# The score fetch of a graph layer: one selection over two PSUM banks, TensorE filling four banks as two pairs

## The chip, the core and the metric

The kernel runs on one core of a Trainium2 chip. The metric is the device time of one execution in microseconds (us), so less is better. TensorE is the engine of the matrix products, VectorE (DVE) works element by element, ScalarE (ACT) computes functions and copies, GpSimd (POOL) here mostly gathers rows, and SyncE (SP) issues transfers. Each runs its own list of instructions in order and waits for the others on counting semaphores.

## The reference

The layer normalizes 3125 node rows of 256 numbers, adds to them a graph attention over 50,000 sorted edges and a second-order attention over all nodes, and ends in a mixture of eight experts of which each row uses two. The graph attention needs, for every edge, a score of its source node and of its destination node in each of four heads:

```python
h = (x @ W).reshape(N, HEADS, HEAD_DIM)
a_src = jnp.einsum('nhd,hd->nh', h, att_src)
a_dst = jnp.einsum('nhd,hd->nh', h, att_dst)
e = a_src[src] + a_dst[dst]
e = jax.nn.leaky_relu(e, NEG_SLOPE)
m = jax.ops.segment_max(e, dst, num_segments=N)
e = jnp.exp(e - m[dst])
```

The change lies in `a_src[src]`: the fetch of 4 source scores for each of 50,176 edges (padded), which the kernel does with matrix products and not with a gather.

## The kernel before

Node scores lie in `tsp`, split into three bf16 parts, with 25 tiles of nodes times 4 heads in the 100 columns. The edges are cut into 128 rows of `EP = 392`; `n` counts these rows. A source index is split into a low part (0 to 127) and a tile number. For a row `n` VectorE has made a one-hot of the low parts (`low_onehots(m)`, L1632, one operation for the 8 rows of group `m`). TensorE multiplies `tsp` by it, three products added up in one PSUM bank (L1180): 100 candidates for each edge, one for every tile and head. VectorE keeps the candidate whose tile is that of the edge and zeroes the others (L1741, the selection, written to one of 8 buffers `mskd`). TensorE then sums the 100 lines to 4 with `rsel` (L1189, `collect`), four rows at a time into quarters of a bank of its own.

TensorE works in 33 turns `i` of `JB = 4` rows: `candidates(i)` fills four banks, `collect(i - 1)` sums the four rows before, and after seven odd turns (`SIDE = (5, 9, 11, 13, 15, 17, 19)`) `side(k)` slips in a small product of another task through bank 5. Candidates rotate over banks 0 to 4: row `n` waits until row `n - 5` is selected (`s_fm`, one count for each selection). `s_fp` counts filled banks, `s_fq` collected turns.

VectorE runs over `n` in order. Ahead of the selections stand other jobs: the one-hot of the next group ahead of row 1 of every group of 8 (`n % FP == 1`), a chain of small operations on slot tables ahead of row 8 (`slot_tables`, L1654 to L1693), a conversion ahead of row 24 (`slot_locals`, L1697 to L1701), and the reading of side product `k` ahead of the row two behind the turn that follows it (`n % JB == 2`; L1706 for k=0, L1708, L1710, five operations L1714 to L1719 for k=3 and k=4, L1725 and L1726 for k=5 and k=6). All these rows `n` are of the form 8j + 2.

After each eight turns ScalarE copies the four sums of a quarter out of PSUM (L944) and SyncE stores them. After the last, SyncE loads all scores back by edge (L735). The scans for the maxima, the projections (L1256) and all that follows come behind the fetch on every engine.

Of the kernel before, what the change touches and what calls it, by code (L numbers as in the profile page):

```python
# [10 lines left out]
ALU = mybir.AluOpType  # L11
# [5 lines left out]
P = 128  # L17
# [3 lines left out]
GH, GD = 4, 64  # L21
MH, MD = 8, 32
NE, HID = 8, 1024
NT = -(-N // P)
# [13 lines left out]
EP = 392  # L38
# [17 lines left out]
JB = 4  # L56
# [67 lines left out]
def gps_layer(nc, x, src, dst, wcat, wgt, att_src, att_dst, gbias, bqkv, wpt, bproj, temp,  # L124
# [6 lines left out]
    def sem(name):  # L131
        return ctx.enter_context(nc.semaphore(name))
# [12 lines left out]
    with ctx:  # L145
# [35 lines left out]
        A = arena[:, :]  # L181
# [4 lines left out]
        def view(base, off, words, pat=None, **kw):  # L186
            v = base[:, off:off + words]
            return v.rearrange(pat, **kw) if pat else v
# [102 lines left out]
        FOFF = RG0  # L291
        FP = 2 * GH
        FM = 2 * JB
# [3 lines left out]
        LB = 4  # L297
        lob = [view(A, AP0 + u * NM // 2, NM // 2).bitcast(BF16) for u in range(LB)]
        hib = [view(A, AP0 + LB * NM // 2 + u * NM // 4, NM // 4).bitcast(U8) for u in range(LB)]
        mskd = [view(A, FOFF + u * EP, EP) for u in range(FM)]  # L300
# [3 lines left out]
        tsp = view(A, o, 3 * NT * GH // 2).bitcast(BF16).rearrange("p (s n) -> p s n", s=3)  # L304
        o += 150
        rsel = view(A, o, 60)
        hi_of = view(A, o + 60, 1)
# [55 lines left out]
        ps = ctx.enter_context(nc.psum_tensor("ps", [P, 8, 512], F32))  # L363
# [67 lines left out]
        s_fp = sem("candidate_scores")  # L431
        s_fm = sem("scores_selected")
# [685 lines left out]
        def _(pe):  # L1118
            MM, TR = nc.tensor.matmul, nc.tensor.transpose
# [7 lines left out]
            for k in range(KD):  # L1127
                for c in range(KD):
                    last = MM(ps[:, 7, k * AH:(k + 1) * AH], wgt_s[:, c, k * P:(k + 1) * P], att_s[:, c, :],
                              start=(c == 0), stop=(c == KD - 1))  # L1130
# [19 lines left out]
            for t in range(NT + 2):  # L1150
                if t < NT:
                    transpose_x(t)
                if t == 2:
                    pe.wait_ge(s_pairb, 1)
                    for c in range(NQC):
                        last = TR(ps[:, 6, c * MD:(c + 1) * MD], pairf[0:MD, c, :], identf[0:MD, 0:MD])
# [13 lines left out]
            def candidates(i):  # L1170

                if i % 2 == 0:
                    pe.wait_ge(s_ohl, i // 2 + 1)
                for c in range(JB):
                    n = i * JB + c
                    if n >= 5:
                        pe.wait_ge(s_fm, n - 4)
                    col = slice((n % FP) * EP, (n % FP + 1) * EP)
                    for s in range(3):
                        last = MM(ps[0:NT * GH, n % 5, 0:EP], tsp[:, s, :], lob[i // 2 % LB][:, col], start=(s == 0), stop=(s == 2))  # L1180
                    last.then_inc(s_fp, 1)

            def collect(i):
                q, k = i // FP, i % FP
                pe.wait_ge(s_fm, (i + 1) * JB)
                if k == 0 and q >= 2:
                    pe.wait_ge(s_fe, q - 1)
                for c in range(JB):
                    last = MM(ps[c * NQ:(c + 1) * NQ, 6 + q % 2, 0:EP], rsel[0:NT * GH, 28 - 4 * k:60 - 4 * k],  # L1189
                              mskd[(i * JB + c) % FM][0:NT * GH, :], start=(k == 0), stop=(k == FP - 1), skip_group_check=True)  # L1190
                last.then_inc(s_fq, 1)
# [26 lines left out]
            for i in range(NQ + 1):  # L1218
                if i < NQ:
                    candidates(i)  # L1220
                if i:
                    collect(i - 1)
                if i in SIDE:
                    side(SIDE.index(i))
            pe.wait_ge(s_w, 16 * 6)
            pe.wait_ge(s_fm, P)
            pe.wait_ge(s_sided, 7)


# [139 lines left out]
            for g in range(KD):  # L1369
                for c in range(NQC):  # L1370
                    last = TR(ps[:, 3 + g, c * P:(c + 1) * P], ftc[g][:, c * P:(c + 1) * P], identf[:, :])
            for c in range(2 * KD):
                last = TR(ps[:, 5, c * P:(c + 1) * P], lcb[:, c * P:(c + 1) * P], identf[:, :])
# [3 lines left out]
            for g in range(KD):  # L1377
                for c in range(NQC):
                    MM(ps[0:MD, 0, g * P:(g + 1) * P], pn[c][:, :], coef[g][:, c * P:(c + 1) * P], start=(c == 0), stop=False)
                last = MM(ps[0:MD, 0, g * P:(g + 1) * P], pn16[:, :], cf16[g], start=False, stop=True)  # L1380
# [75 lines left out]
            for n in range(ZR + 1):  # L1456
                r, c = n // NQC, n % NQC
# [44 lines left out]
            for k in range(TOPK):  # L1502
                pe.wait_ge(s_slots, k + 1)
                for t in range(NT):
                    n = P if t < NT - 1 else TAIL
                    last = MM(ps[:, 3, 0:2 * NJ], lo1[k][0:n, t, :], slotv[k][0:n, t, :, :].rearrange("p v j -> p (v j)"),
                              start=(k == 0 and t == 0), stop=(k == TOPK - 1 and t == NT - 1))
# [40 lines left out]
        def _(dve):  # L1548
            V = nc.vector
# [80 lines left out]
            def low_onehots(m):  # L1630
                dve.wait_ge(s_lol[m % LB], 32 * (m // LB) + 32)
                V.tensor_scalar(lob[m % LB], lob[m % LB], iota_p[:, 0:1], None, ALU.is_equal).then_inc(s_ohl, 1)  # L1632
# [62 lines left out]
            def slot_locals():  # L1695
                dve.wait_ge(s_slg, 16 * 4)
                V.tensor_copy(fsrc, sl_src)  # L1697
                for u in range(2):
                    ins = V.tensor_scalar(fdl[:, u, :], sl_dst[:, u, :], tsm[:, u:u + 1], None, ALU.subtract)
                st(ins)  # L1700
                V.tensor_copy(fdlb, fdl).then_inc(s_slf, 1)  # L1701

            def side(k):
                dve.wait_ge(s_side, k + 1)
                if k == 0:
                    V.tensor_copy(ts_row[:, :], ps[0:1, 5, 0:NSP]).then_inc(s_sided, 1)  # L1706
                if k == 1:
                    V.tensor_copy(adT[0:NT, :], ps[0:NT, 5, :]).then_inc(s_sided, 1)  # L1708
                if k == 2:
                    V.tensor_copy(tselT[0:NT, :], ps[0:NT, 5, 0:2 * P]).then_inc(s_sided, 1)  # L1710
                if k in (3, 4):
                    v = ps[:, 5, 0:2 * NS].rearrange("p (h s) -> p h s", h=2)
                    q = [dslot[:, s, 2 * (k - 3):2 * (k - 2), :] for s in range(3)]
                    st(V.tensor_copy(q[0], v))  # L1714
                    V.tensor_tensor(dres, v, q[0], ALU.subtract).then_inc(s_sided, 1)
                    dve.wait_ge(s_sided, k + 1)
                    st(V.tensor_copy(q[1], dres))
                    st(V.tensor_tensor(dres, dres, q[1], ALU.subtract))
                    st(V.tensor_copy(q[2], dres))  # L1719
                if k in (5, 6):  # L1720
                    u = k - 5
                    n = min(P, NS - u * P)
                    v = ps[:, 5, :].rearrange("p (w k s) -> p w k s", w=2, k=TE)
                    o, e = u * P * TE, (u * P + n) * TE
                    V.tensor_copy(tsrc[:, o:e].rearrange("p (s k) -> p k s", k=TE), v[:, 0, :, 0:n])  # L1725
                    V.tensor_copy(tdl[:, o:e].rearrange("p (s k) -> p k s", k=TE), v[:, 1, :, 0:n]).then_inc(s_sided, 1)  # L1726
            for n in range(P):
                m = n // FP
                if n % FP == 1 and m + 1 < P // FP:
                    low_onehots(m + 1)  # L1730
                if n == CHAIN:
                    slot_tables()
                if n == 3 * FP:
                    slot_locals()
                if n % JB == 2 and n // JB - 1 in SIDE:
                    side(SIDE.index(n // JB - 1))
                dve.wait_ge(s_fp, n + 1)
                if n >= FM:
                    dve.wait_ge(s_fq, n // JB - 1)
                e = n % FP  # L1740
                V.scalar_tensor_tensor(mskd[n % FM][0:NT * GH, :], hib[m % LB][0:NT * GH, e * EP:(e + 1) * EP], hi_of[0:NT * GH, 0:1],  # L1741
                                       ps[0:NT * GH, n % 5, 0:EP], ALU.is_equal, ALU.mult).then_inc(s_fm, 1)


            dve.wait_ge(s_w, 16 * 6)
# [258 lines left out]
            for n in range(ZR + 1):  # L2004
                r, c = n // NQC, n % NQC
# [206 lines left out]
```

## Time and profile before

| | us |
|---|---|
| median of 3 runs | 1489.79 |
| lowest and highest run | 1482.92, 1490.13 |
| the profiled execution, own time | 1487.99 |
| its span | 1486.0 |
| busy in the span: TensorE, VectorE, GpSimd | 1219.2, 903.5, 760.8 |
| the fetch: first and last instruction of L1180 and L1189 | 69.4 to 182.0 |

The span runs from the first to the last instruction; 2.0 us of the execution lie around it. The shares of busy time are averages over stages with different limits, so what is said of the fetch is read from its own 113 us. TensorE has two clocks, 1.2 and 2.4 GHz; PEclk gives the granted share of the higher one.

### The profile page before, as it was taken

Reading aid. Unit: us, or ns where it says so; the run is one execution under the profiler, and the core shown is the slowest. Engines: PE = TensorE matmul, PEld = TensorE weight load, DVE = VectorE, ACT = ScalarE, POOL = GpSimd, SP = SyncE. Lnnn points to the kernel's source line nnn. Section 1 sums busy time; section 2 is a strip of 40 time slices with the busy share of each in tenths; the row PEclk is TensorE's granted clock in tenths of the full one; section 3 lists DMA queues with packets and bytes.
Section 4 is the critical chain, followed back from the end, with each engine's and each line's share of the span. In section 5 each row is a group of like instructions: output and inputs, shape, how many; then the busy total and the mean of one; then the engine's idle time right before and its main releaser. Section 6 shows DMA issues by size and latency. Waiting matters only on the chain.

```text
span 1486.0 us, 24323 instructions
## 1 busy us (share of the span) xinstructions
PE 1219.2 (82%) x7992; PEld 872.4 (59%) x7993; DVE 903.5 (61%) x1752; ACT 392.8 (26%) x1067; POOL 760.8 (51%) x630
## 2 busy tenths in 40 slices
PE   3789946757778876699999998354899999999995
PEld 2645523435445544445555555244899999999994
DVE  8589879789989987566656555686322333333321
ACT  1300011421111110144343341132233333333331
POOL 1070000888888887777777777550133333333331
PEclk9889967878889888999999999655899999999998
DMA  5535374322222223343333333674022222222223
GB/s 176 203 122 188 140 291 141 118 82 72 68 75 76 71 70 90 103 118 99 114 111 110 112 100 113 273 261 152 22 36 36 36 35 35 35 35 35 38 38 102
DMA packets 67562, 153.61 MB, mean 103 GB/s; under 512 B 12961, under 2 KB 41558, under 8 KB 66262
## 3 DMA queue, kind: packets, MB, share of 16 engines
q0 software_dynamic: 32640, 75.27, 20.6%
q1 hardware_dynamic: 33478, 74.93, 14.3%
q10 hardware_dynamic: 1360, 2.33, 0.4%
q8 instruction: 47, 0.77, 0.2%
q14 instruction: 37, 0.30, 0.1%
HBM read 131.76 MB, written 23.92 MB: 105 GB/s over the span
## 4 chain that ended last, share of the span: by engine, by line
PE 56%; DVE 21%; POOL 10%; issue 6%; DMA 5%; DVEq 1%; ACT 1%; SPq 0%; POOLq 0%; ACTq 0%
PE ps L1531 13%; PE ps L1541 12%; PE ps L1239 11%; POOL arena L845 9%; DVE arena L1797 6%; PE ps L1180 4%; PE ps L1435 2%; PE ps L1447 2%; PE ps L1189 2%; PE ps L1268 1%; DMA arena<-h_d,tables 1%; PE ps L1147 1%; DMA h_d<-arena 1%; DMA acc<-xn_d,tables 1%; PE ps L1393 1%
## 5 line engine op out<-in xcount | busy, mean ns | idle before, releaser
L845 POOL DMA_INDIRECT arena<-h_d,tables x440 | 536.5, 1219 | 134.0 <-issue 128.9
L1239 PE MATMUL ps<-arena 128*128 128x264 f32 x880 | 255.2, 446 | 93.0 <-DVE acc L1806 77.2
L1239 PEld LDWEIGHTS ps<-arena 128*128 128x128 f32 x880 | 186.8, 221 | 154.1 <-issue 88.1
L887 POOL DMA_INDIRECT sum_d<-acc,tables x56 | 89.9, 1605 | 253.6 <-DVE acc L2171 246.0
L1531 PE MATMUL ps<-acc 128*128 128x128 f32 x1792 | 211.4, 277 | 0.0
L1531 PEld LDWEIGHTS ps<-acc 128*128 128x128 f32 x1792 | 206.5, 193 | 0.3
L1541 PE MATMUL ps<-arena,acc 128*128 x896 | 202.5, 379 | 0.0
L1541 PEld LDWEIGHTS ps<-arena,acc 128*128 128x128 f32 x896 | 166.1, 190 | 20.3
L1821 DVE TENSOR_TENSOR arena<-arena 128x1024 f32<-128x1024 f32 x110 | 134.3, 1221 | 67.8 <-DMA arena<-h_d,tables 67.3
L1109 ACT ACTIVATE acc<-ps,b_s 128x128 f32<-128x128 f32 x448 | 127.7, 368 | 120.5 <-PE ps L1531 120.5
L1055 ACT ACTIVATE arena<-ps 128x1024 f32<-128x1024 f32 (+1 forms) x112 | 98.3, 929 | 218.9 <-PE ps L1435 218.9
L2159 DVE COPY acc<-arena 128x1024 f32 x112 | 79.5, 710 | 122.5 <-PE ps L1531 121.9
L2168 DVE TENSOR_TENSOR acc<-ps,arena 128x256 f32<-128x256 f32 x56 | 23.8, 424 | 163.8 <-PE ps L1541 163.8
L1797 DVE TENSOR_TENSOR arena<-arena 128x1920 f32<-128x1920 f32 x50 | 107.5, 2154 | 22.3 <-PE ps L1275 22.3
L1806 DVE TENSOR_TENSOR acc<-acc,ps 128x264 f32 x220 | 93.1, 423 | 40.0 <-PE ps L1239 27.6
L879 POOL DMA_INDIRECT acc<-xn_d,tables x56 | 58.5, 1044 | 83.8 <-DVE tables L2149 67.0
L1180 PE MATMUL ps<-arena 128*100 128x392 bf16 x384 | 76.2, 349 | 9.9 <-DVE arena L1741 8.2
L851 POOL DMA_INDIRECT acc<-max_d,small x2 | 3.8, 1882 | 147.6 <-DMA max_d<-acc 147.3
L1256 PE MATMUL ps<-arena 128*128 128x512 f32 (+1 forms) x200 | 78.4, 538 | 0.0
L1741 DVE SCALAR_TENSOR_TENSOR arena<-arena,ps 100x392 f32<-100x392 uint8 x128 | 71.8, 615 | 10.2 <-PE ps L1180 10.1
L1816 DVE TENSOR_TENSOR arena<-iota_f,tables 128x512 f32<-128x512 f32 x110 | 75.2, 684 | 0.0
L1180 PEld LDWEIGHTS ps<-arena 128*100 128x100 bf16 x384 | 47.8, 132 | 43.3 <-DVE arena L1741 18.7
(363 smaller groups left out, 1426.4 us busy)
## 6 DMA issues: line engine op xcount, KB each, us to landing
arena<-dl_d SPq DMA_DIRECT2D x22, 640.0 KB, 6.6
arena<-lo_d SPq DMA_DIRECT2D x16, 784.0 KB, 4.5
arena<-h_d,tables POOLq DMA_INDIRECT x440
arena<-in_w SPq DMA_DIRECT2D x4, 1664.0 KB, 12.2
arena<-in_w SPq DMA_DIRECT2D x4, 1632.0 KB, 24.4
arena<-hi_d SPq DMA_DIRECT2D x16, 343.0 KB, 5.1
h_d<-arena SPq DMA_DIRECT2D x25, 128.0 KB, 2.5
sum_d<-res SPq DMA_DIRECT2D x5, 640.0 KB, 6.3
```

The source lines that it names most:

```text
L845: pool.indirect_dma_start(gb[u][:, k, 0:D], None, h_d, bass.IndirectOffsetOnAxis(tsrc[:, j:j + 1], 0)).then_inc(s_gg[u], 16)
L887: pool.indirect_dma_start(sum_d, bass.IndirectOffsetOnAxis(pidx[:, j:j + 1], 0), ys[j % 2], None, compute_op=ALU.add).then_inc(s_fy, 16)
L1055: A_.activation(zsq[n % 2][:, 2 * half:2 * half + 2, 0:w], ps[:, 2 * half:2 * half + 2, 0:w], ACT.Square)\
L1109: last = A_.activation(hT[u][:, c, :], ps[:, 1 + 2 * u + n_, (c % 4) * P:(c % 4 + 1) * P], ACT.Relu, bias=b1_s[:, ds(ej * HC + c, 1)])
L1180: last = MM(ps[0:NT * GH, n % 5, 0:EP], tsp[:, s, :], lob[i // 2 % LB][:, col], start=(s == 0), stop=(s == 2))
L1239: last = MM(ps[:, 6 + s, 0:ACOL], oh[b % OB][:, m, :], gb[u][:, m, :], start=(k == 0), stop=(k == TE - 1))
L1531: last = MM(ps[:, 1 + 2 * (u % 2) + n_, c * P:(c + 1) * P], w1c[n_][:, k, c * P:(c + 1) * P], xfT[u % 2][:, k, :], start=(k == 0), stop=(k ...
L1541: last = MM(ps[:, 5 + u % 2, 0:D], hT[u % 2][:, c, :], w2_s[:, ds(e, 1), c, :].rearrange("p o n -> p (o n)"), start=(c == 0), stop=(c == H ...
L1797: V.tensor_tensor(phi[g].rearrange("p h (r i) -> p h r i", i=MD)[:, :, 1:SQ], k0, k1, ALU.mult).then_inc(s_phi, 1)
L1806: V.tensor_tensor(q, q, ps[:, 6 + s, 0:ACOL], ALU.add).then_inc(s_accd, 1)
L1821: V.tensor_tensor(v, v, over(wm[:, m:m + SB * TE, 0:GH], GD), ALU.mult).then_inc(s_msg, 1)
L2159: V.tensor_copy(w1c[n_], w1_s[:, ds(e, 1), :, n_ * HH:(n_ + 1) * HH].rearrange("p o k n -> p (o k) n"))\
```

## The change

A selection (now L1742) covers two rows: it reads two neighbouring PSUM banks and writes two neighbouring `mskd` buffers, 784 elements in place of 392. TensorE uses banks 0 to 3 as two pairs, waits once for a pair and fills both banks; `s_fm` counts pairs. The one-hots of the next group move from ahead of row 1 to ahead of row 2, which is the second pair of the group.

```diff
                 for c in range(JB):
                     n = i * JB + c
-                    if n >= 5:
-                        pe.wait_ge(s_fm, n - 4)
+                    if c % 2 == 0 and n >= 4:
+                        pe.wait_ge(s_fm, n // 2 - 1)
                     col = slice((n % FP) * EP, (n % FP + 1) * EP)
                     for s in range(3):
-                        last = MM(ps[0:NT * GH, n % 5, 0:EP], tsp[:, s, :], lob[i // 2 % LB][:, col], start=(s == 0), stop=(s == 2))
+                        last = MM(ps[0:NT * GH, n % 4, 0:EP], tsp[:, s, :], lob[i // 2 % LB][:, col], start=(s == 0), stop=(s == 2))
                     last.then_inc(s_fp, 1)
 
             def collect(i):
                 q, k = i // FP, i % FP
-                pe.wait_ge(s_fm, (i + 1) * JB)
+                pe.wait_ge(s_fm, (i + 1) * JB // 2)
...
-            pe.wait_ge(s_fm, P)
+            pe.wait_ge(s_fm, P // 2)
...
-            for n in range(P):
+            for n in range(0, P, 2):
                 m = n // FP
-                if n % FP == 1 and m + 1 < P // FP:
+                if n % FP == 2 and m + 1 < P // FP:
                     low_onehots(m + 1)
...
-                dve.wait_ge(s_fp, n + 1)
+                dve.wait_ge(s_fp, n + 2)
                 if n >= FM:
                     dve.wait_ge(s_fq, n // JB - 1)
                 e = n % FP
-                V.scalar_tensor_tensor(mskd[n % FM][0:NT * GH, :], hib[m % LB][0:NT * GH, e * EP:(e + 1) * EP], hi_of[0:NT * GH, 0:1],
-                                       ps[0:NT * GH, n % 5, 0:EP], ALU.is_equal, ALU.mult).then_inc(s_fm, 1)
+                two = view(A, FOFF + n % FM * EP, 2 * EP, "p (k e) -> p k e", k=2)
+                V.scalar_tensor_tensor(two[0:NT * GH], hib[m % LB][0:NT * GH, e * EP:(e + 2) * EP].rearrange("p (k e) -> p k e", k=2),
+                                       hi_of[0:NT * GH, 0:1], ps[0:NT * GH, n % 4:n % 4 + 2, 0:EP], ALU.is_equal, ALU.mult)\
+                    .then_inc(s_fm, 1)
```

On TensorE the products stay the same in number and order; their waits change. One turn before, from the turn behind side product 1 (the names in brackets are the semaphores waited for; `scores_selected` is `s_fm`):

```order
L1180 MATMUL ps<-arena 100x392 [waits scores_selected,low_onehots]
L1180 MATMUL ps<-arena 100x392 x2
L1180 MATMUL ps<-arena 100x392 [waits scores_selected]
L1180 MATMUL ps<-arena 100x392 x2
L1180 MATMUL ps<-arena 100x392 [waits scores_selected]
L1180 MATMUL ps<-arena 100x392 x2
L1180 MATMUL ps<-arena 100x392 [waits scores_selected]
L1180 MATMUL ps<-arena 100x392 x2
L1189 MATMUL ps<-arena 32x392 [waits scores_selected]
L1189 MATMUL ps<-arena 32x392 x3
```

The same turn after:

```order
L1180 MATMUL ps<-arena 100x392 [waits scores_selected,low_onehots]
L1180 MATMUL ps<-arena 100x392 x5
L1180 MATMUL ps<-arena 100x392 [waits scores_selected]
L1180 MATMUL ps<-arena 100x392 x5
L1189 MATMUL ps<-arena 32x392 [waits scores_selected]
L1189 MATMUL ps<-arena 32x392 x3
```

Four waits, each for one bank, have become two, each for a pair of banks. On VectorE, around the reading of side product 3 (L1714 to L1719), before:

```order
L1632 TENSOR_SCALAR arena<-arena,iota_p 128x3136
L1741 SCALAR_TENSOR_TENSOR arena<-arena,ps 100x392
L1714 CAST arena<-ps 128x440
L1715 TENSOR_TENSOR arena<-ps,arena 128x440
L1717 CAST arena<-arena 128x440
L1718 TENSOR_TENSOR arena<-arena 128x440
L1719 CAST arena<-arena 128x440
L1741 SCALAR_TENSOR_TENSOR arena<-arena,ps 100x392 x7
```

And there after:

```order
L1632 TENSOR_SCALAR arena<-arena,iota_p 128x3136
L1714 CAST arena<-ps 128x440
L1715 TENSOR_TENSOR arena<-ps,arena 128x440
L1717 CAST arena<-arena 128x440
L1718 TENSOR_TENSOR arena<-arena 128x440
L1719 CAST arena<-arena 128x440
L1742 SCALAR_TENSOR_TENSOR arena<-arena,ps 100x784 x4
```

The selection that stood between the one-hots and the side product is gone: both now stand together between the first and the second pair of the group.

## Rows read from the trace of the kernel before

**Rows 1.** Chain of waits in order of time: start, duration, work (us).
```profile
157.72 2.12 PE ps L1180 x12
159.85 0.80 PE ps L1189 x8
...
182.05 0.49 ACT arena L944
```

**Rows 2.** Stages: length, busy time and count by engine, PEclk, DMA share.
```profile
core 0: us, PE busy (x) PEld busy (x) DVE busy (x) ACT busy (x) POOL busy (x), PEclk, DMA share, GB/s
...
86.00:88.00 2.00, 1.91 (x6) 1.08 (x6) 2.00 (x5) 0.00 (x0) 1.39 (x3) 0.50 0.25 66
...
132.00:140.00 8.00, 6.39 (x45) 3.45 (x44) 7.52 (x14) 0.48 (x1) 0.00 (x0) 1.00 0.31 114
140.00:160.00 20.00, 20.00 (x140) 11.20 (x142) 19.10 (x35) 0.00 (x0) 0.00 (x0) 1.00 0.56 197
```

**Rows 3.** Line L1741: duration in ns, then TensorE's total wait for it.
```profile
L1741 DVE SCALAR_TENSOR_TENSOR arena<-arena,ps x128: 600/617/624, 70.7 to 180.4; 100x392 f32<-100x392 uint8 x128
...
  PE ps L1180: 8.2, 6
```

**Rows 4.** Timeline (start, length, instructions), slot tables and after.
```profile
77.14 0.18 DVE L1654 COPY small<-ps 128x32 f32<-128x32 f32 x1
...
83.94 0.62 DVE L1741 SCALAR_TENSOR_TENSOR arena<-arena,ps 100x392 f32<-100x392 uint8 x1
...
84.61 0.70 PE L1180 MATMUL ps<-arena 128*100 128x392 bf16 x3 [3.77 <-DVE arena L1741]
...
86.09 2.20 PE L1180 MATMUL ps<-arena 128*100 128x392 bf16 x6 [0.78 <-DVE arena L1741]
```

**Rows 5.** Timeline, the conversion ahead of row 24.
```profile
96.78 0.42 DVE L1697 CAST acc<-acc 128x512 f32<-128x512 int32 x1
...
99.45 0.61 DVE L1741 SCALAR_TENSOR_TENSOR arena<-arena,ps 100x392 f32<-100x392 uint8 x1
...
101.60 0.70 PE L1180 MATMUL ps<-arena 128*100 128x392 bf16 x3 [0.24 <-DVE arena L1741]
...
102.45 0.70 PE L1180 MATMUL ps<-arena 128*100 128x392 bf16 x3 [0.15 <-DVE arena L1741]
```

**Rows 6.** Timeline, side product 4.
```profile
134.33 0.61 DVE L1714 CAST arena<-ps 128x440 bf16<-128x440 f32 x1
...
137.12 3.92 DVE L1741 SCALAR_TENSOR_TENSOR arena<-arena,ps 100x392 f32<-100x392 uint8 x7
137.80 0.70 PE L1180 MATMUL ps<-arena 128*100 128x392 bf16 x3 [1.61 <-DVE arena L1741]
```

**Rows 7.** Timeline of an undisturbed group.
```profile
157.66 2.19 PE L1180 MATMUL ps<-arena 128*100 128x392 bf16 x12
158.39 0.62 DVE L1741 SCALAR_TENSOR_TENSOR arena<-arena,ps 100x392 f32<-100x392 uint8 x1 [0.53 <-PE ps L1180]
158.93 1.03 DVE L1632 TENSOR_SCALAR arena<-arena,iota_p 128x3136 bf16<-128x3136 bf16 x1
159.88 3.82 DVE L1741 SCALAR_TENSOR_TENSOR arena<-arena,ps 100x392 f32<-100x392 uint8 x7
```

**Rows 8.** Two other sizes of operation on VectorE.
```profile
L1982 DVE SCALAR_TENSOR_TENSOR arena<-ps,sk,arena 128x512 f32<-128x512 f32 x12 | 9.0, 748 | 9.6 <-PE ps L1403 9.6
...
L2159 DVE COPY acc<-arena 128x1024 f32 x112 | 79.5, 710 | 122.5 <-PE ps L1531 121.9
```

**Rows 9.** Timeline, side product 1 and the first copy of side product 5.
```profile
112.92 0.67 DVE L1708 COPY arena<-ps 25x512 f32<-25x512 f32 x1
...
142.44 0.42 DVE L1725 CAST tables<-ps 128x256 int32<-128x256 f32 x1
```

**Rows 10.** Chain of waits in order of time, behind the slot tables.
```profile
88.28 1.46 PE ps L1189 x8
89.75 3.42 PE ps L1180 x12
```

## Prediction

> **What bounds the kernel now.** I read the page first, then the chain of waits, then the busy time by stage, and last the timeline of the fetch. In the chain the undisturbed part of the fetch is TensorE alone: 2.12 us for the twelve products of a turn, 0.80 us for the collecting ones, then the next turn, so 2.92 us a turn [rows 1]. The stages say the same: from 140 to 160 us TensorE is busy for 20.00 of 20 us at the full clock. VectorE is close behind with 19.10 of 20 [rows 2]. VectorE sets the pace only where it has another job in between. In the whole fetch TensorE waits 8.2 us for selections, in six waits [rows 3]: 3.77 and 0.78 behind the slot tables [rows 4], 0.24 and 0.15 behind the conversion [rows 5], 1.61 each behind side products 3 and 4, of which the second is shown [rows 6].
>
> The end of the fetch is the start of all that follows: ScalarE's last copy comes at 182.05 [rows 1], then the store, the load by edge, the scans. All engines run their lists in order and none has work there that could take up a delay, so I count a microsecond of the fetch as one of the kernel.
>
> **The change, part by part.** TensorE's products stay the same, so its 2.92 us a turn stay. What can change are its waits. The change takes VectorE time away and coarsens the hand-over.
>
> *Cost of a selection.* Seven in a row take 3.82 us [rows 7] at 0.617 each [rows 3], so the next starts (3.82 - 0.62) / 6 = 0.53 after the one before; 0.08 overlap. For 392 more elements I take the slope of the same operation: 748 ns at 512 wide against 617 at 392 is 1.09 ns an element [rows 3, 8], so 0.617 + 0.43 = 1.04 us for a pair, called d, and 0.96 to the next start. 64 pairs save VectorE 64 x (1.07 - 0.96) = 7 us. No row shows this operation over two banks. The upper bound is two single ones, 1.23; as lower bound I take 0.71, the copy of 1024 elements [rows 8], which has no PSUM operand. The same operation at 512 is by far the nearest, so 1.04 stands.
>
> *One undisturbed group (two turns, four pairs).* Time 0 is the first product of the group. A bank (three products) shows on VectorE 0.73 later (157.66 to 158.39 [rows 7]). Products follow each other by 0.163 (twelve in 2.12 with 0.33 for the last), so a pair shows at 0.73 + 0.49 = 1.22. VectorE is free then (it waits there today, 0.53 [rows 7]). It selects the first pair, is free at 1.22 + d - 0.08, makes the one-hots of the next group (0.95 to the next start, 158.93 to 159.88 [rows 7]), and selects the second pair until 2.09 + 2d. TensorE sees that 0.06 later (137.12 + 0.62 to 137.80 [rows 6]). It wants the same two banks again for the second pair of the second turn, at 2.92 + 6 x 0.163 = 3.90. So it waits w = 2d - 1.75 = 0.33 us. Today there is no such wait: the selection of the second edge row follows the one-hots in 0.62, banks come free one by one, and five of them carry TensorE over the rest. In the second turn VectorE catches up (two pairs, 1.9 us, in 2.92), so the wait comes once in each group and no lateness is carried on. Nothing else is queued behind TensorE's wait than its own next products; the one-hots for the next group are done at about 3.2, due at 5.8. SyncE's loads of index parts hang on collected turns and only move back with them.
>
> Six groups are of this plain kind (of the 16, the first has no banks to wait for, the last makes no one-hots, and eight have other jobs): 6 x 0.33 = 2.0 us.
>
> *Groups with side product 1, 2, 5 or 6.* Their reading now stands directly behind the one-hots, ahead of the second pair, so its whole length adds to w. A copy 512 wide takes 0.67, one 256 wide 0.42 [rows 9], and by that slope one 184 wide 0.35. That is 0.67 (side 1), 0.42 (2), twice 0.42 (5), twice 0.35 (6): 2.63, less six overlaps of 0.08, 2.15. Wait 4 x 0.33 + 2.15 = 3.5 us, today none.
>
> *Side products 3 and 4.* Five operations hold VectorE for 137.12 - 134.33 = 2.79 [rows 6]. TensorE then waits 0.33 + 2.79 = 3.12 in place of 1.61: 2 x 1.51 = 3.0 us more.
>
> *Slot tables.* They start when the selection of edge rows 6 and 7 ends, 0.42 later than today, and so end at 83.94 + 0.42 = 84.36. Edge rows 8 and 9 are selected until 85.40, TensorE fills edge rows 12 and 13 from 85.46. Today it had edge row 12 done already and filled 13 at 84.61. It runs at the lower clock there (0.50 [rows 2]), six products at 0.327 each: edge row 14 starts at about 87.4 in place of 86.09 [rows 4], 1.3 us more.
>
> *Conversion ahead of edge row 24, then one-hots and side product 0 ahead of edge row 26.* It starts 0.42 later, at 97.20, and ends 2.67 later [rows 5], at 99.87. Pair 24 holds VectorE until 100.83, one-hots until 101.78, the 256-wide copy (0.34) until 102.12, pair 26 until 103.16. Edge rows 30 and 31 go at 103.22. Today 31 alone goes at 102.45 [rows 5]: 103.22 + 0.49 - 102.45 = 1.3 us more.
>
> *The end.* The last collect waits for a pair that shows 2.20 after its turn began, so until 2.20 + 1.04 + 0.06 = 3.30, and is due at 2.92: 0.4 us.
>
> Sum: 2.0 + 3.5 + 3.0 + 1.3 + 1.3 + 0.4 = 11.5 us more. With d = 0.71, w vanishes in the plain groups and the sum is 0.8 (sides 1, 2, 5, 6) + 1.7 (sides 3 and 4) + 0.7 + 0.3 + 0.1 = 3.6. With d = 1.23, w is 0.71 and it is 4.3 + 5.0 + 3.8 + 1.9 + 1.9 + 0.6 = 17.5. A gain of the fetch is left out even at the lower bound.
>
> *TensorE's clock.* It fell to the lower of its two levels after the 3.77 us wait (PEclk 0.50 from 86 to 88) and stayed at the higher one through the 1.61 us wait near 137 (1.00 from 132 to 140) [rows 2, 4, 6]. The new waits of 3.12 us lie between the two, nearer to the first. A fall cost the turn behind the tables 1.46 in place of 0.80 for the collect and 3.42 in place of 2.12 for the products [rows 1, 10], 1.96 us, of which the slower products cover one w: 1.6 us net. I take one fall.
>
> The profiled execution took 1487.99 us (span 1486.0 and 2.0 around it): 1487.99 + 11.5 + 1.6 = 1501.1 us. From the median of the runs, 1.8 higher, it would be 1502.9.
>
> VectorE's share bears on one rule. At 19.10 busy of 20 us beside TensorE's 20.00 [rows 2] it is nearly full, yet TensorE is the one that never rests. The Trainium skill, Perfetto Trace Analysis, section "Optimizing Scalar/DVE Operations", says that grouping into larger operations helps where the engine is saturated, and that where it is not, but makes others idle, breaking operations up may let work finish sooner. By its first half the 7 us that VectorE saves would come back as a gain (the last rival); by its second half the change goes the wrong way, which is what the group above gives.
>
> **The rivals.**
> - *The pair is much cheaper than its width, or VectorE starts it sooner than I think.* For it: nothing in the rows but that the operation is unseen over two banks. Against: the same operation at 512 wide. At d = 0.71 it gives 1487.99 + 3.6 = 1491.6.
> - *The second bank costs a whole operation more.* For it: only that no row of VectorE crosses banks. Two singles, d = 1.23: 1487.99 + 17.5 = 1505.5, with two falls of the clock 1508.7.
> - *VectorE is the engine that decides, and its 7 us are a gain* (the other side). Place: the six waits of 8.2 us [rows 3]. If the shorter selections let VectorE reach each disturbance early and TensorE's four full banks outlast it, all six go: 1487.99 - 8.2 = 1479.8. The point from which it decides is d below (1.75 - job) / 2, where job is what stands between the pairs: 0.87 for the plain group, nothing above zero for 2.79. Against it: the large waits come from jobs, not from selections.
>
> **How the numbers follow.** A time difference of 0.5% is 7.4 us, about what a measurement of this kernel tells from none. Forecast 0.62, its own range 1496 to 1505; the cheap pair 0.20, within 0.5%; the dear pair 0.12; the gain 0.06. So faster 0.06, same 0.20, slower 0.74. The range runs from 1490 to 1508: it takes in the cheap pair's 1491.6 and most of the dear one.
>
> **What would show it.** The selection line should have 64 instructions of about 1.04 us. TensorE's wait for it should grow from 8.2 to some 19 us, with one wait of about 0.3 in each plain group, once in 6.2 us in place of 5.84, and two of about 3.1; the last collect should be some 11 to 14 us later. VectorE's busy time in the fetch should fall by some 5 to 7 us. I am wrong if TensorE runs through the plain groups without a wait (then one-hots or pairs are shorter than taken), or if later stages take the delay back.

## The result, and the profile after

The change made the kernel slower: 1497.3 us, median of 6 runs (1495.22 to 1499.11), against 1489.47 (1482.92 to 1490.13, 6 runs); ratio 1.0061, 95% interval 1.0042 to 1.0081, which is 6 to 12 us. Forecast were 1501.1, that is 13.1 us more, and a range of 1490 to 1508. The profiled execution took 1495.22, its span 1493.1: 7.2 and 7.1 more than before.

The selection's line of the kernel after: its duration in ns (min/median/max), what VectorE idled for ahead of it, and who waited for it. It answers to [rows 3].

```profile
L1742 DVE SCALAR_TENSOR_TENSOR arena<-arena,ps x64: 1008/1030/1032, 69.7 to 187.9; 100x784 f32<-100x784 uint8 x64
its engine sat idle before it (us, times) until:
  PE ps L1180: 25.2, 31
...
  PE ps L1180: 14.8, 10
```

The idling of VectorE in the same view of the kernel before (L1741):

```profile
  PE ps L1180: 10.1, 16
```

A pair takes 1.030 us (1.04 was taken), and the products wait 14.8 us for pairs in place of 8.2. VectorE's busy time in the fetch fell from 101.5 us (68 to 182) to 94.5 (68 to 190), the 7 us of the working. They were no gain: VectorE now idles 25.2 us for products in place of 10.1, 15.1 more, about the 7 us saved and the 8.9 by which the fetch is longer.

TensorE's timeline of the kernel after: start, length, instructions, and in brackets the idle time ahead with its releaser. It answers to [rows 4 to 7].

```profile
74.60 2.19 PE L1180 MATMUL ps<-arena 128*100 128x392 bf16 x12
...
82.73 4.00 PE L1180 MATMUL ps<-arena 128*100 128x392 bf16 x12 [5.14 <-DVE arena L1742]
...
99.81 1.20 PE L1180 MATMUL ps<-arena 128*100 128x392 bf16 x6 [1.02 <-DVE arena L1742]
...
129.62 1.20 PE L1180 MATMUL ps<-arena 128*100 128x392 bf16 x6 [2.89 <-DVE arena L1742]
130.75 1.51 PE L1189 MATMUL ps<-arena 100*32 100x392 f32 x8
132.19 1.83 PE L1210 MATMUL ps<-arena 25*128 25x220 f32 x4
133.95 4.00 PE L1180 MATMUL ps<-arena 128*100 128x392 bf16 x12
...
141.96 1.20 PE L1180 MATMUL ps<-arena 128*100 128x392 bf16 x6 [2.09 <-DVE arena L1742]
...
158.24 2.19 PE L1180 MATMUL ps<-arena 128*100 128x392 bf16 x12
161.17 2.48 PE L1180 MATMUL ps<-arena 128*100 128x392 bf16 x12
164.37 2.19 PE L1180 MATMUL ps<-arena 128*100 128x392 bf16 x12
```

The last three rows are a plain group (one without a side product or other job) and the start of the next: from 158.24 to 164.37 it lasts 6.13 us in place of 5.84. The 0.29 shows as no wait at all. It sits inside the second turn, whose twelve products take 2.48 in place of 2.19. Elsewhere, too, a wait shown is about 0.2 shorter than the delay, so delays below are taken from start to start.

The chain of waits of the kernel after, in order of time, where [rows 1] had TensorE alone:

```profile
158.31 1.14 PE ps L1180 x6
...
160.42 0.91 DVE arena L1632
161.33 0.04 issue
161.37 1.04 DVE arena L1742
162.40 0.04 issue
162.45 1.20 PE ps L1180 x6
```

The path leaves TensorE after the first pair of a group, goes over the one-hots (L1632) and the selection behind them (L1742), and comes back to TensorE with the next pair of products. That is the loop from which w = 2d - 1.75 was worked out.

Stages of the kernel after, columns as in [rows 2]:

```profile
80.00:82.00 2.00, 0.00 (x0) 0.00 (x0) 1.90 (x7) 0.00 (x0) 1.15 (x1) 0.50 0.95 365
...
88.00:90.00 2.00, 2.00 (x18) 1.16 (x16) 1.30 (x2) 0.00 (x0) 2.00 (x3) 1.00 0.09 33
...
132.00:136.00 4.00, 4.00 (x15) 2.50 (x12) 0.00 (x0) 0.00 (x0) 0.00 (x0) 0.50 0.00 0
...
140.00:160.00 20.00, 16.68 (x113) 9.22 (x114) 15.29 (x20) 0.00 (x0) 0.00 (x0) 1.00 0.54 184
```

From 140 to 160 us TensorE is down from 20.00 to 16.68 and VectorE from 19.10 to 15.29: neither is full. The clock fell behind side product 3 (0.50 from 132 to 136), which it had not done before.

### The profile page after: what moved, and what is told of

It reads as the page before. It is cut to its first block, busy times and chain, and to the rows that moved or that the text cites. A ratio compares the mean times of both kernels' runs of the same rounds, so it can differ in the third digit from the quotient of the medians.

```text
span 1493.1 us, 24199 instructions
## 1 busy us (share of the span) xinstructions
PE 1220.8 (82%) x7992; PEld 872.3 (58%) x7993; DVE 895.5 (60%) x1688; ACT 393.1 (26%) x1067; POOL 757.6 (51%) x630
## 4 chain that ended last, share of the span: by engine, by line
PE 56%; DVE 22%; POOL 9%; issue 5%; DMA 4%; DVEq 1%; ACT 1%; SPq 0%; POOLq 0%; ACTq 0%
PE ps L1531 13%; PE ps L1541 12%; PE ps L1239 11%; POOL arena L845 8%; DVE arena L1799 5%; PE ps L1180 3%; PE ps L1435 2%; PE ps L1447 2%; DVE arena L1742 1%; DMA h_d<-arena 1%; PE ps L1268 1%; PE ps L1393 1%; DMA arena<-h_d,tables 1%; DVE arena L1759 1%; DVE res L2072 1%
## 5 line engine op out<-in xcount | busy, mean ns | idle before, releaser
L1239 PE MATMUL ps<-arena 128*128 128x264 f32 x880 | 259.5, 452 | 90.2 <-DVE acc L1808 74.2
L1180 PE MATMUL ps<-arena 128*100 128x392 bf16 x384 | 76.4, 345 | 17.3 <-DVE arena L1742 14.8
L1742 DVE SCALAR_TENSOR_TENSOR arena<-arena,ps 100x784 f32<-100x784 uint8 x64 | 65.0, 1027 | 25.3 <-PE ps L1180 25.2
```

The lines of the kernel that those rows point to most:

```text
L1180: last = MM(ps[0:NT * GH, n % 4, 0:EP], tsp[:, s, :], lob[i // 2 % LB][:, col], start=(s == 0), stop=(s == 2))
L1239: last = MM(ps[:, 6 + s, 0:ACOL], oh[b % OB][:, m, :], gb[u][:, m, :], start=(k == 0), stop=(k == TE - 1))
```

## The experiments

Theory A is the prediction's: four banks handed over in pairs, with a job of VectorE between two pairs, make TensorE wait. Its rivals put the loss on one thing alone: the number of banks, the wide instruction itself, or the place of the one-hots. Two lengths are read from each trace: the fetch (first product to last collect), and the fetch from its first collect on. The second leaves out the first two turns, which ran at either clock from trace to trace (5.3 to 7.0 us for the same 24 products; e7 and e9, whose products and waits there are the same, took 5.96 and 6.98) and say little of the change.

| kernel | banks | hand-over | one-hots ahead of | fetch | from first collect | median (runs) | ratio to before, 95% |
|---|---|---|---|---|---|---|---|
| before | 5 | single | row 1 | 112.53 | 105.56 | | |
| after | 4 | pair | row 2 | 121.41 | 116.08 | 1497.3 (6) | 1.0061, 1.0042 to 1.0081 |
| e1 | 6 | pair | row 2 | 112.61 | 106.92 | 1485.73 (10) | 0.9995, 0.9977 to 1.0012 |
| e2 | 4 | single | row 1 | 115.81 | 108.81 | 1489.33 (10) | 1.0021, 1.0007 to 1.0035 |
| e3 | 4 | pair, narrow | row 2 | 127.24 | 120.65 | 1501.74 (4) | 1.0115, 1.0092 to 1.0138 |
| e4 | 4 | pair | row 4 | 112.94 | 105.93 | 1486.56 (10) | 1.0004, 0.9992 to 1.0017 |
| e5 | 5 | single | row 4 | 109.16 | 103.24 | 1482.98 (10) | 0.9967, 0.9951 to 0.9983 |
| e6 | 6 | pair | row 4 | 109.80 | 103.16 | 1484.19 (10) | 0.9968, 0.9954 to 0.9982 |
| e7 | e5, slot tables ahead of the fetch | | | 101.31 | 95.35 | 1476.45 (6) | 0.9921, 0.9895 to 0.9947 |
| e8 | e6, slot tables ahead of the fetch | | | 102.64 | 95.67 | 1475.98 (6) | 0.9913, 0.9893 to 0.9932 |
| e9 | e7, GpSimd's additions later | | | 102.47 | 95.49 | 1479.62 (6) | 0.9934, 0.9915 to 0.9953 |

Before was run again beside each batch: 1486.48 with e1 to e4, 1488.08 with e5 to e8, 1488.13 with e9.

**e1: three pairs of banks.** The kernel after with six banks for candidates. The side products move to bank 7, and the collects use bank 6 alone.

```diff
-                    if c % 2 == 0 and n >= 4:
-                        pe.wait_ge(s_fm, n // 2 - 1)
+                    if c % 2 == 0 and n >= 6:
+                        pe.wait_ge(s_fm, n // 2 - 2)
...
-                        last = MM(ps[0:NT * GH, n % 4, 0:EP], ...
+                        last = MM(ps[0:NT * GH, n % 6, 0:EP], ...
```

> The changed kernel with three pairs of banks in place of two (side products and collects moved to the two banks left). The fetch, from the first L1180 to the end of the last L1189, lasted 112.5 us before and 121.3 after. Theory A (TensorE has too little lead: with two pairs it must have the second pair back while VectorE still makes one-hots or reads a side product): with a third pair the wait of 0.29 us in the plain groups goes to zero, the waits behind side products 3 and 4 fall from 3.1 and 2.3 to about 1.7 each, and the fetch lasts 112 to 113.5 us, the kernel within 2 us of before. Rival B (the wide selection itself costs, by its length or by the second bank, however many banks there are): the plain groups keep their wait and the fetch lasts 119 to 122 us.

Two plain turns and the waits for side products 3 and 4 on TensorE's timeline of e1, then one of its stages:

```profile
127.16 0.87 PE L1189 MATMUL ps<-arena 100*32 100x392 f32 x8 [1.89 <-DVE arena L1742]
...
135.90 0.87 PE L1189 MATMUL ps<-arena 100*32 100x392 f32 x8 [1.89 <-DVE arena L1742]
...
162.66 2.19 PE L1180 MATMUL ps<-arena 128*100 128x392 bf16 x12
...
165.58 2.19 PE L1180 MATMUL ps<-arena 128*100 128x392 bf16 x12
```

```profile
136.00:140.00 4.00, 4.00 (x20) 2.47 (x21) 2.08 (x3) 0.00 (x0) 0.00 (x0) 0.62 0.62 249
```

Turns are 2.92 us again, with the wide selections kept. From the first collect on 1.4 us of the 10.5 are left, and the clock fell behind the second of these waits. That the whole fetch is as long as before is luck: its first two turns took 5.69 us for 6.97. So the wide instruction itself costs nothing: what it costs is lead. The waits for side products 3 and 4 have moved to the collects.

**e2: four single banks.** The kernel before with one bank fewer.

```diff
-                    if n >= 5:
-                        pe.wait_ge(s_fm, n - 4)
+                    if n >= 4:
+                        pe.wait_ge(s_fm, n - 3)
```

> The kernel before with four single banks in place of five; selections stay single and hand back one bank each. Theory A (the hand-over by pairs costs most): only the longest jobs outlast one bank less, plain groups stay at 5.84 us, the fetch lasts 114 to 116 us (about 3 over before). Rival C (the fifth bank is what was lost, pairs or not): the fetch lasts 120 us or more, as after.

It came out at 115.81. If the number of banks alone did it, it would be at after's 121. From the first collect on, the lost bank costs 3.3 us of after's 10.5, and part of the 3.3 is a fall of the clock behind a wait of 2.11:

```profile
127.57 1.37 PE L1180 MATMUL ps<-arena 128*100 128x392 bf16 x6 [2.11 <-DVE arena L1741]
```

```profile
128.00:132.00 4.00, 4.00 (x17) 1.66 (x15) 2.18 (x5) 0.00 (x0) 0.00 (x0) 0.57 0.20 77
```

The first fence is TensorE's timeline of e2, the second its stages. Plain groups have no wait with four single banks.

**e3: pairs handed over, but selected one by one.** The kernel after with two selections of 392, of which the second gives the signal.

```diff
-                two = view(A, FOFF + n % FM * EP, 2 * EP, "p (k e) -> p k e", k=2)
-                V.scalar_tensor_tensor(two[0:NT * GH], ...).then_inc(s_fm, 1)
+                for j in range(2):
+                    ins = V.scalar_tensor_tensor(mskd[(n + j) % FM][0:NT * GH, :], ...)
+                ins.then_inc(s_fm, 1)
```

> The changed kernel with each wide selection made as two single ones that still wait for and hand back a pair of banks together. Theory A: a pair now takes VectorE 1.15 us in place of 1.03, so w = 2 x 1.15 - 1.75 = 0.55 in each group in place of 0.3, and the fetch lasts 123 to 126 us, 3 us longer than after. Rival B (the wide selection itself costs): the fetch falls back towards 113 us.

TensorE's timeline of e3, one plain group:

```profile
162.88 2.19 PE L1180 MATMUL ps<-arena 128*100 128x392 bf16 x12
...
167.34 1.20 PE L1180 MATMUL ps<-arena 128*100 128x392 bf16 x6 [0.34 <-DVE arena L1742]
...
169.27 2.19 PE L1180 MATMUL ps<-arena 128*100 128x392 bf16 x12
```

The group lasts 6.39, so w is 0.55; with d = 1.15 (two selections) the formula gives 2 x 1.15 - 1.75 = 0.55. The fetch was a little longer than expected: behind a wait of 3.14 the clock was at half from 132 to 140. Between e3 and after only the width differs: 120.65 against 116.08, so the wide selection by itself is a gain of 4.6 us here. A part of it is clock: in after it was at half from 132 to 136 only, 4 us less. Between e2 and e3 (108.81 and 120.65) it is the grain of the signal, with the one-hots a row later: a loss of 11.8, the clock's falls included.

**e4: the one-hots later.** The kernel after with the one-hots of the next group ahead of its third pair, so no longer together with the side products.

```diff
-                if n % FP == 2 and m + 1 < P // FP:
+                if n % FP == 4 and m + 1 < P // FP:
```

> The changed kernel with the one-hots of the next group ahead of the third pair of each group in place of the second, so that they no longer stand in front of the same pair as the side products. Theory A: the third pair has a whole collect and the fill of another pair as slack; the wait in the plain groups goes to zero, side products 1, 2, 5 and 6 wait less than 0.3 each, 3 and 4 about 2, and the fetch lasts 113 to 115 us. Rival D (the place of the one-hots does not matter, since VectorE's work per group is the same): 121 us as after.

One number undoes the loss, with four banks and pairs kept. Plain groups have no wait, nor have side products 1, 2, 5 and 6; at 3 and 4 it is 2.00 and 1.95, and the clock did not fall there (TensorE's timeline and stages of e4; the last three rows of the timeline are a plain group of 5.84 us):

```profile
127.87 1.20 PE L1180 MATMUL ps<-arena 128*100 128x392 bf16 x6 [2.00 <-DVE arena L1742]
...
157.23 2.19 PE L1180 MATMUL ps<-arena 128*100 128x392 bf16 x12
...
160.15 2.19 PE L1180 MATMUL ps<-arena 128*100 128x392 bf16 x12
...
163.07 2.19 PE L1180 MATMUL ps<-arena 128*100 128x392 bf16 x12
```

```profile
128.00:132.00 4.00, 4.00 (x26) 2.33 (x26) 2.67 (x4) 0.00 (x0) 0.00 (x0) 1.00 0.32 121
```

So the place of the one-hots isn't the cause by itself either: e1 has them where after has, and loses little. Most of the loss needs all three: four banks, pairs, and the one-hots ahead of the second pair, with the side product's reading behind them. Of the 10.5 us, 1.4 are left without the first (e1), 3.3 without the second (e2), 0.4 without the third (e4).

**e5 and e6: the same edit with five single banks and with three pairs.** e5 is the kernel before, e6 is e1, each with this one line (e5's is shown, e6 had `== 2`).

```diff
-                if n % FP == 1 and m + 1 < P // FP:
+                if n % FP == 4 and m + 1 < P // FP:
```

> The kernel before (five single banks) with only the one-hots of the next group moved from ahead of row 1 to ahead of row 4 of each group, as in the run that made the pairs as good as before. Theory A (what costs is how much VectorE work stands in front of one hand-over; the one-hots and a side product in one place add up): the waits behind side products 3 and 4 fall from 1.61 to about 0.7 to 1 each and the two near row 30 vanish, 2 to 3 us off the fetch, 110 us. Rival (with single banks the place is covered already by the five banks): 112.5 us as before.

> Three pairs of banks and the one-hots ahead of the third pair. Theory A: waits behind side products 3 and 4 about 0.9 each in place of 1.9, fetch 110 us, 2 to 3 below before. Rival (three pairs already cover all that banks can cover): 112.5 us as the three pairs alone.

Both are faster than before and equal to each other from the first collect on (103.24 and 103.16). TensorE's timeline of e5 at side products 3 and 4:

```profile
126.50 0.70 PE L1180 MATMUL ps<-arena 128*100 128x392 bf16 x3 [0.67 <-DVE arena L1741]
...
134.51 0.70 PE L1180 MATMUL ps<-arena 128*100 128x392 bf16 x3 [1.02 <-DVE arena L1741]
```

These two waits were 1.61 each [rows 3, 6], and the two behind the conversion [rows 5] are gone. What is left is the wait for the slot tables, 4.79.

**e7 and e8: the slot tables ahead of the fetch.** e5 and e6 with `slot_tables` called ahead of the splitting of the scores, and the product that it waits for put among the last products of the stage before. One wait more inside `slot_tables` (for `s_xt`) is not shown.

```diff
+                if t == NT - 3:
+                    pe.wait_ge(s_off, 1)
+                    MM(ps[:, 7, 256:288], onesf[:, :], cnt, start=True, stop=True).then_inc(s_offp, 1)
...
-            pe.wait_ge(s_off, 1)
-            MM(ps[:, 7, 256:288], onesf[:, :], cnt, start=True, stop=True).then_inc(s_offp, 1)
...
+            slot_tables()
             dve.wait_ge(s_nas, NT)
...
-                if n == CHAIN:
-                    slot_tables()
```

> The five single banks with the one-hots ahead of row 4, and the slot tables (6.8 us of small VectorE operations ahead of row 8) taken out of the fetch, into the time in which VectorE waits for the last node scores (13.4 us idle before L1644 in the trace of before); the small product that they need goes ahead on TensorE too. Theory A: the wait of 3.77 + 0.78 us goes and with it the fall of the clock behind it (2.0 us); fetch about 103 us, the kernel 8 to 11 us below before, 1476 to 1480. Rival (the tables end late, or another transfer is late next): less than 4 us gained.

> The same with three pairs of banks and wide selections. Theory A: TensorE is the bound once no job stands in front of a hand-over, so VectorE's 7 us of shorter selections buy nothing more: the fetch lasts 103 us like the five singles, within 1 us. Rival (VectorE is the bound there): 2 us or more below the five singles.

These are the fastest kernels here. In the fetch of e7 only the waits of 0.67 and 1.03 are left. e7 and e8 agree within their intervals and, from the first collect on, to 0.3 us: with the waits gone TensorE sets the pace in both, and the wide selections' saving buys nothing. VectorE's stage row shows where it went (e7 first, then e8):

```profile
140.00:160.00 20.00, 20.00 (x140) 11.02 (x140) 18.69 (x33) 0.48 (x1) 0.00 (x0) 1.00 0.60 193
```

```profile
140.00:160.00 20.00, 20.00 (x139) 10.72 (x138) 17.08 (x18) 0.49 (x1) 0.00 (x0) 1.00 0.54 191
```

TensorE is full in both. VectorE only rests more in e8.

**e9: GpSimd's additions behind the splitting.** In e7 the fetch began 3.27 us after TensorE's last work, where before it was 1.78; the splitting of the scores ran beside additions of GpSimd. e9 is e7 with one wait ahead of these.

```diff
+            pool.wait_ge(s_prep, 2)
             st(pool.tensor_tensor(bres_s, bres_s, bres2, ALU.add))
```

> The five singles with one-hots at row 4 and early slot tables, where GpSimd's additions (L829, L831) now also wait until VectorE has split the node scores (L1692 to L1697). In the run before, three of those five small operations took 0.62 to 0.72 us in place of 0.21 to 0.26, while GpSimd added. Theory P (VectorE's operations on SBUF are slowed by GpSimd's running beside them): all five take 0.21 to 0.28 again and the fetch starts 1.3 us sooner after the last node score, 1.3 us off the kernel. Rival (they were slow for another reason, the DMA or the earlier place of the tables): they stay at 0.6 to 0.7 us. The fetch itself lasts 101 to 103 us by both.

VectorE's timeline of e7 and then of e9, the splitting and the conversion, and behind e7's the additions on GpSimd's timeline:

```profile
66.35 0.26 DVE L1692 CAST arena<-nas 128x100 bf16<-128x100 f32 x1 [4.12 <-ACT nas L932]
66.64 0.28 DVE L1693 TENSOR_TENSOR dif<-nas,arena 128x100 f32<-128x100 f32 x1
66.95 0.72 DVE L1694 CAST arena<-dif 128x100 bf16<-128x100 f32 x1
67.70 0.69 DVE L1695 TENSOR_TENSOR dif<-dif,arena 128x100 f32<-128x100 f32 x1
68.43 0.62 DVE L1697 CAST arena<-dif 128x100 bf16<-128x100 f32 x1
...
88.00 0.61 DVE L1703 TENSOR_SCALAR acc<-acc,small 128x256 f32<-128x256 int32 x2
```

```profile
66.08 0.72 POOL L829 TENSOR_TENSOR arena<-arena 128x256 f32<-128x256 f32 x1
66.88 20.00 POOL L831 TENSOR_TENSOR res<-res,arena 128x256 f32<-128x256 f32 x25
```

```profile
69.26 0.21 DVE L1695 CAST arena<-dif 128x100 bf16<-128x100 f32 x1
69.50 0.26 DVE L1696 TENSOR_TENSOR dif<-dif,arena 128x100 f32<-128x100 f32 x1
69.80 0.21 DVE L1698 CAST arena<-dif 128x100 bf16<-128x100 f32 x1
...
89.97 1.54 DVE L1704 TENSOR_SCALAR acc<-acc,small 128x256 f32<-128x256 int32 x2
```

The three operations are back at 0.21 to 0.26, so the slowness was GpSimd's company. e8 says the same against the rival: with the tables as early as in e7 it made the three at 0.21 to 0.26, for its additions began only at 69.26, while the last of them ran. The whole splitting takes 1.34 us in place of 2.70. Now the conversion, later in the fetch, runs beside the additions and takes 1.54 in place of 0.61, where no product waits for it. It did so in the kernel before too (1.55), and there the two waits of [rows 5] lay behind it. The kernel did not get faster (0.9934, interval 0.9915 to 0.9953, against e7's 0.9921, 0.9895 to 0.9947). A gain of 1.4 us is inside these intervals, so this is inconclusive for the time, and conclusive only for the cause of the slow operations.

## Why the prediction was right, point by point

**What bounds.** Right: the fetch ends 189.88 - 181.98 = 7.9 us later, the span is 7.1 longer and the medians differ by 7.8. Little or nothing behind the fetch took the delay back; the interval of the ratio is too wide to say more.

**The selection.** 64 of 1.030 us, against 1.04: the slope within one bank holds over two. The cheap and the dear pair are out.

**The plain group.** 0.29 for 0.33, six times: 1.75 us for 2.0. Shown three ways: the chain, e3 with the other d, and e1 and e4, which take the wait away, one by a third pair and one by moving the one-hots.

**Side products 1, 2, 5, 6.** Delays from start to start of 0.89, 0.63, 0.97 and 0.82: 3.3 us for 3.5.

**Side products 3 and 4.** The first is 3.10 for 3.12. The second is 2.30 only: behind the first the clock had fallen, and products at half speed wanted the banks later. e3 had the same pattern (3.14 and 2.20 shown), and e4, where the clock stayed, had 2.00 and 1.95. By this measure before's 1.61 are 1.84 each, so the two add 1.26 + 0.47 = 1.7 us in place of 3.0. Here the working failed in size, twice: it priced the second disturbance as if the first had left no trace, and it subtracted waits as the trace shows them from delays counted from start to start.

**Slot tables, conversion, end.** 12.07 us from the products at 74.60 to the next collect, before 11.0: 1.1 for 1.3. The conversion cost 1.1 for 1.3, the last collect 0.3 for 0.4.

**The clock.** One fall more, as said, behind side product 3. Collect, side product and the twelve products there took 137.88 - 130.75 = 7.13 us, at the full clock 0.80 + 0.93 + 2.12, so 3.28 more. Against this the turn behind the tables, at the full clock again by 88 us, saved 1.97. Net 1.3 for 1.6, and that the two are so near is luck: the new fall cost twice the 1.6 taken for it. What was not foreseen is that the old fall moved: in after the clock fell during the longer wait at the tables, and it was back a turn earlier.

Together 9.2 of waits (forecast 11.5) and 1.3 of clock (1.6) give 10.5, and the fetch from its first collect on is 10.5 longer. So of the 13.1 us forecast 2.6 were too much, half of it at side products 3 and 4. Another 2.6 lie ahead of the first collect and were no part of the working: after's first two turns took 5.33 us for 6.97, so that its fetch was 8.9 longer in all, and it began 1.0 earlier. These two differ from trace to trace and are not shown to come from the change. They hold for the two profiled executions; the medians can't be split so.

**The signs.** Two of those named came out smaller: TensorE's wait rose to 14.8 us and not to 19, as the waits in plain groups show as none, the others 0.2 short, and that for side product 4 was smaller; and the last collect came 7.9 later and not 11 to 14.

**The rival that VectorE decides.** Refuted at its own point: the 7 us were saved, and VectorE's idling for products rose from 10.1 to 25.2 us. e8 against e7 shows the same where nothing else waits. The Trainium skill, Perfetto Trace Analysis, section "Optimizing Scalar/DVE Operations", gives two halves: larger operations where the engine is saturated, smaller ones where it makes others idle. The second half is what this kernel followed: with four banks the fetch from its first collect on lasts 108.81 us with single selections (e2) and 116.08 with wide ones. e3 adds a reservation: breaking up the operation while the signal still comes once for two is the slowest of all (1.0115 against 1.0061). It was the signal that had to be finer, not the instruction.

## What to carry to other kernels

A wider operation on the consumer's side frees its buffers later and in larger lumps: count, for one period, when the producer wants the lump back, and put every job that the consumer does in between into that count. If it comes out positive, add a lump of lead or move the jobs to where the consumer is ahead, before merging instructions. In this kernel an engine at 95% busy, for which another never waits in its plain stretches, gave nothing when it was relieved; moving one job by a few rows, and another out of the loop, gave what the merging did not (0.9921 with single selections, 0.9913 with wide ones).

## What the runs showed of the hardware that was not expected

- One VectorE operation over two PSUM banks (784 of 2 x 512 elements) takes 1.030 us; one bank takes 0.617. The second bank costs its elements and nothing else that shows.
- Operations of VectorE on 128x100 took 0.62 to 0.72 us in place of 0.21 to 0.26 beside GpSimd's additions (25 in 20.00 us, most of them 0.72 long); two of the conversion took 1.54 together in place of 0.61. The selections, which read one operand from PSUM, took 0.62 either way. The Trainium skill, SBUF — State Buffer, section "Who interferes with whom", says that an operation of VectorE with at most one SBUF input and outside the two-port modes does not contend with GpSimd, and that otherwise whichever is issued second waits for the other to finish. For the three slow operations of e7 the rows agree: L1694 ended at 67.67, and the addition beside which it began would be done at 66.88 + 0.72 = 67.60. L1693, with two SBUF inputs, does not fit: it took 0.28 beside the first addition (66.08 to 66.80), against 0.26 in e9 with no addition running. L1692 took 0.26 there, and no row shows whether it ran in such a mode. Why these two were not slowed is open.
- The length of a wait alone does not tell whether the clock falls. It fell behind waits of 2.11 (e2), 2.89 (after) and 3.14 (e3), and stayed behind 1.61 (before), 2.00 (e4), 2.09 (after) and 2.20 (e3, 1.00 from 144 to 152); of e1's two waits of 1.89 one was followed by a fall (0.62 from 136 to 140) and one was not. What decides between them is open.
